# A gnn and mixture-of-experts kernel: tokens laid 32 to a partition, x loaded in five pieces, z made by two engines, rows filled in advance in longer runs

## The reference

```
z   = layernorm(x)
agg = adj @ z + beta[:, None] * z                  # adj is 4096 x 4096, float32, 64 MiB
x   = x + (agg / (sum(adj, axis=1) + beta)[:, None]) @ kernel + bias
z1  = layernorm(x)
logits = z1 @ Wr + br;  top 2 of 64;  gates = softmax of the two logits
x   = x + sum over the two: gate * (relu(z1 @ W1[e] + b1[e]) @ W2[e] + b2[e])
```

## Time and profile before

| | us |
|---|---|
| median of the three runs | 433.78 |
| the profiled execution | 433.03 |
| its span, first to last instruction | 431.2 |
| TensorE, VectorE, GpSimd, ScalarE busy | 359.3, 312.4, 250.3, 157.8 |

### The profile page before, as it was taken

One profiled execution on the slowest core, in us unless ns is written; L12 is line 12 of the kernel. 1 busy time (PEld: TensorE's weight loads), 2 busy tenths in 40 slices (PEclk: granted clock), 3 DMA queues, 4 the chain that ended last, 5 costly groups with the idle time before them and its releaser, 6 DMA issues.

```text
span 431.2 us, 8273 instructions
## 1 busy us (share of the span) xinstructions
PE 359.3 (83%) x2029; PEld 286.2 (66%) x2029; DVE 312.4 (72%) x891; ACT 157.8 (37%) x242; POOL 250.3 (58%) x226
## 2 busy tenths in 40 slices
PE   5899699996999999999899935289999999999300
PEld 2334486784786877868678632179999999999300
DVE  2699779859789798898897628246777767677257
ACT  1115185454384654845738030001222112122054
POOL 4377600308488585884857763517777777777700
PEclk8799899996999999999999975869999999999955
DMA  8998999899696996969955110479999999997189
GB/s 267 351 423 280 338 364 357 240 361 397 249 397 218 420 366 234 401 214 403 374 218 238 44 46 19 142 205 269 307 295 311 304 285 312 295 277 235 31 288 297
DMA packets 59653, 119.32 MB, mean 277 GB/s; under 512 B 7656, under 2 KB 36604, under 8 KB 51440
## 3 DMA queue, kind: packets, MB, share of 16 engines
q1 hardware_dynamic: 41968, 95.95, 63.8%
q10 hardware_dynamic: 12672, 14.58, 11.0%
q0 software_dynamic: 4992, 8.54, 5.5%
HBM read 104.09 MB, written 16.78 MB: 280 GB/s over the span
## 4 chain that ended last, share of the span: by engine, by line
PE 33%; POOL 19%; DVE 17%; DMA 15%; issue 10%; ACT 3%; SPq 1%; ACTq 0%; POOLq 0%; DVEq 0%
POOL dispatched_rows L451 14%; PE bank L897 8%; DMA dispatched_rows<-payload,slot 7%; PE bank L907 4%; PE bank_pair L907 4%; DVE z_sb L600 4%; DVE adj_low L615 3%; POOL diag L438 3%; DMA x_sb<-x 3%; DMA expert_answers<-adj_ring,ans 3%; PE bank L891 2%; PE bank L843 2%; PE bank L839 2%; PE bank_pair L904 2%; PE bank L840 2%
## 5 line engine op out<-in xcount | busy, mean ns | idle before, releaser
L615 DVE TENSOR_TENSOR adj_low<-adj_ring,adj_high 128x2048 fp32r<-128x2048 f32 x49 | 114.3, 2347 | 24.5 <-ACT adj_high L501 24.2
L451 POOL DMA_INDIRECT dispatched_rows<-payload,slot x64 | 95.7, 1495 | 37.8 <-issue 31.3
L501 ACT CAST adj_high<-adj_ring 128x2048 fp32r<-128x2048 f32 x49 | 93.4, 1907 | 60.7 <-PE bank L843 47.6
L470 POOL DMA_INDIRECT expert_answers<-adj_ring,ans x92 | 90.5, 983 | 41.4 <-ACT adj_ring L551 21.8
L839 PE MATMUL bank<-adj_high,z_hi 128*128 128x512 f32 x196 | 80.7, 412 | 0.0
L840 PE MATMUL bank<-adj_high,z_lo 128*128 128x512 f32 x196 | 77.5, 396 | 0.0
L749 DVE TENSOR_SCALAR adj_ring<-bank,adj_ring 128x128 f32<-128x128 f32 x184 | 56.1, 346 | 16.4 <-PE bank L897 13.2
L829 PE MATMUL bank<-adj_ring,z_sb 128*128 128x512 f32 x120 | 58.2, 629 | 5.5 <-DVE z_sb L600 5.3
L897 PE MATMUL bank<-xt_sb,adj_ring 128*128 128x128 f32 x368 | 57.6, 280 | 0.2 <-DVE xt_sb L739 0.2
L843 PE MATMUL bank<-adj_low,z_hi 128*128 128x512 f32 x196 | 53.5, 395 | 0.0
L897 PEld LDWEIGHTS bank<-xt_sb,adj_ring 128*128 128x128 f32 x368 | 49.7, 196 | 0.5 <-DVE xt_sb L739 0.5
(11 more groups left out here) (125 smaller groups left out, 452.8 us busy)
## 6 DMA issues: line engine op xcount, KB each, us to landing
adj_ring<-adj_t SPq DMA_DIRECT2D x64, 1024.0 KB, 8.4
adj_ring<-w_pack SPq DMA_DIRECT2D x48, 257.5 KB
adj_ring<-w_pack ACTq DMA_DIRECT2D x44, 257.5 KB
dispatched_rows<-pad_row SPq DMA_DIRECT2D x8, 528.0 KB, 9.8
adj_ring<-expert_answers SPq DMA_DIRECT2D x8, 512.0 KB, 7.3
adj_ring<-dispatched_rows SPq DMA_DIRECT2D x48, 66.0 KB
adj_ring<-dispatched_rows ACTq DMA_DIRECT2D x44, 66.0 KB
out<-x_sb SPq DMA_DIRECT2D x8, 256.0 KB, 5.2
```

Of the source, the lines that this page charges most:

```text
L451: pool.indirect_dma_start(rows, bass.IndirectOffsetOnAxis(ap=slot[:, b, i:i + 1], axis=0), payload[:, b, t, k, :], None).then_inc(scattere ...
L470: pool.indirect_dma_start(y_tok, bass.IndirectOffsetOnAxis(ap=ans[:, s:s + 1], axis=0), y_sb[:, s, :], None, bounds_check=N * K - 1, oob_i ...
L501: nc.scalar.copy(high[:, m % PARTS], adj_sb[:, slot_of(g, k)]).then_inc(hi_ready, 1)
L615: v.tensor_tensor(low[:, m % PARTS], adj_sb[:, slot_of(g, k)], high[:, m % PARTS].bitcast(F32), ALU.subtract).then_inc(lo_ready, 1)
```

## The change

A token is now `p * 32 + t`: each partition holds 32 tokens that follow one another in DRAM. x, beta, the answers and the output are read and written so, and the adjacency is laid out for it on the host (same runs of 8192 bytes). An expert's answer index follows (`answer_tab`).

x comes in five pieces of 4, 4, 8, 8 and 8 tiles (`BATCHES`), one run to a partition each. Pieces 1 and 2 are issued behind adjacency chunk 0, piece 3 behind chunk 1, piece 4 behind chunk 2. VectorE does statistics of piece b + 1 before the z of piece b. It makes the z of the first half of each piece, ScalarE that of the other half, from `rstd0` and `shift0`. VectorE no longer waits for `consts` at the start, and ScalarE takes one square root ahead of time, so that its table is loaded.

GpSimd no longer adds the bias to x. The bias is loaded into row 127 of a zeroed tile and added to the weight, whose last row meets the column of ones. The order of GpSimd's constants changes.

The rows filled in advance are now written in runs of eight (4224 bytes). Each of the eight DMAs covers 64 partitions, one to an expert, with two runs each, by turns from partitions 0 to 63 and 64 to 127. Their places among the chunks (`PADS`) stay.

```diff
+BATCHES = ((0, 4), (4, 4), (8, 8), (16, 8), (24, 8))
+X_BEFORE = (1, 3, 4, 5)
...
-            x_tiles = x.rearrange("(t p) f -> p t f", p=P)
-            sp.dma_start(x_sb[:, 0:GT], x_tiles[:, 0:GT]).then_inc(x_first, 16)
+            x_tiles = x.rearrange("(p t) f -> p t f", p=P)
+            def load_x(b):
+                first, count = BATCHES[b]
+                sp.dma_start(x_sb[:, first:first + count], x_tiles[:, first:first + count]).then_inc(x_in[b], 16)
+            load_x(0)
...
-                if k == 0:
-                    sp.dma_start(x_sb[:, GT:TILES], x_tiles[:, GT:TILES]).then_inc(x_in, 16)
+                if k < len(X_BEFORE) - 1:
+                    for b in range(X_BEFORE[k], X_BEFORE[k + 1]):
+                        load_x(b)
...
-                    sp.dma_start(gnn_b_sb[:], gnn_b.partition_broadcast(P)).then_inc(params_in, 16)
+                    sp.dma_start(gnn_b_sb[P - 1:P, :], gnn_b.partition_broadcast(1)).then_inc(params_in, 16)
...
-                        sp.dma_start(first_rows[:, padded:padded + EC],
-                                     pad_row[:, None, :].to_broadcast([P, EC, ROW])).then_inc(prefilled, 16)
+                        start = padded // PAD_BLOCKS % 2 * E
+                        sp.dma_start(blocks[:, padded:padded + PAD_BLOCKS],
+                                     pad_rows[start:start + E, None, :].to_broadcast([E, PAD_BLOCKS, PAD_RUN * ROW])).then_inc(prefilled, 16)
...
-            for g in range(GROUPS):
-                add_bias(g)
-                if g < SPLIT:
-                    low_z(g)
+            for g in range(SPLIT):
+                low_z(g)
+            pool.wait_ge(params_in, 16 * 5)
...
+            def make_z(b):
+                act.wait_ge(shift0, b + 1)
+                for t in act_half(b):
+                    nc.scalar.activation(z_sb[:, t, 0:D - 1], x_sb[:, t, 0:D - 1], ACT.Identity,
+                                         bias=shift0_sb[:, t:t + 1], scale=rstd0[:, t:t + 1]).then_inc(z_by_act, 1)
...
+            root_z(0)
+            for b in range(len(BATCHES)):
+                make_z(b)
+                if b + 1 < len(BATCHES):
+                    root_z(b + 1)
+                high_z(b)
...
+            spread_x(0)
+            for b in range(len(BATCHES)):
+                if b + 1 < len(BATCHES):
+                    spread_x(b + 1)
+                make_z(b)
...
+            own.after(v.tensor_tensor(gnn_wd[:, 0:D], gnn_w_sb[:], wrow_ps[:, 0:D], ALU.subtract))
+            v.tensor_tensor(gnn_wd[:, 0:D], gnn_wd[:, 0:D], gnn_b_sb[:], ALU.add).then_inc(wd_ready, 1)
```

More of the change, by code:

```diff
@@ L50, with batch_of, dve_half, act_half @@
 RING = 5
+BATCHES = ((0, 4), (4, 4), (8, 8), (16, 8), (24, 8))
+X_BEFORE = (1, 3, 4, 5)
 OUT_CH = 4
 OUT_STEPS = TILES // OUT_CH
+def batch_of(j):
+    return max(b for b, (first, _) in enumerate(BATCHES) if first <= j)
+def dve_half(b):
+    first, count = BATCHES[b]
+    return range(first, first + count // 2)
+def act_half(b):
+    first, count = BATCHES[b]
+    return range(first + count // 2, first + count)
+def z_made(j):
+    b = batch_of(j)
+    earlier = BATCHES[b][0] // 2
+    if j in dve_half(b):
+        return "dve", earlier + j - dve_half(b)[0] + 1
+    return "act", earlier + j - act_half(b)[0] + 1
 def chunk_no(g, k):
@@ L210, in program @@
         y_in = in_ring(TILES * K * D, "p (t k f) -> p t k f", t=TILES, k=K)
-        x_first = sem("x_first")
-        x_in = sem("x_in")
+        x_in = [sem(f"x_in{b}") for b in range(len(BATCHES))]
         params_in = sem("params_in")
@@ L346, in _ @@
             sp.wait_ge(consts, 1)
-            first_rows = rows.rearrange("(e s) c -> s e c", e=E)[0:P]
+            blocks = rows.rearrange("(e s r) c -> e s (r c)", e=E, r=PAD_RUN)
             padded = 0
@@ L399, in _ @@
             pool.memset(seen[:], 0.0)
-            pool.memset(eps_sb[:], EPS)
-            own.after(pool.memset(payload[:], 0.0))
-            pool.memset(pad_row[:, ANSWER:ANSWER + 1], float(NO_ANSWER))
+            own.after(pool.memset(payload[:, :, :, :, ANSWER + 1:ROW], 0.0))
             pool.affine_select(out=ident[:], in_=ident[:], compare_op=ALU.not_equal, fill=1.0, base=0,
@@ L786, in _ @@
             warm(14, spare_bank)
-            pe.wait_ge(consts, 1)
+            pe.wait_ge(z_ones, 1)
             def gnn(g):
```

117 lines of the change are left out of this document (65 added, 52 removed).

## The result

The changed kernel takes **420.57 us** (median of four executions, 419.54 to 421.76); the kernel before took 433.39 on the same chip. The ratio is 0.9705, 95% interval 0.9672 to 0.9738, so 12.8 us faster. The forecast was 418.0 with a range of 413.8 to 425.5. The profiled execution took 419.54 us, its span is 417.7 us, 13.5 less than before.

A forecast was written before the change was run, and what follows sets the result against it. Group 0 was bound by the layernorm, z and `diag` chain, later groups mostly by TensorE, group 2 by a late DMA chunk. Terms -8.9 - 1.2 - 4.9 - 0.8 = -15.8 us took 433.78 to 418.0 us, range 413.8 to 425.5.

The forecast's parts named there:

- Start unchanged: Group 0: TensorE's start stays at 9.48 us, first chunk at low clock until about 15.4, then own product at 39.8.
- Rival (c): Group 0: z makers and `z_lo` collide, TensorE ends at 44 us as now; 422 to 423 us in all, chance 0.09.
- The copy at 40.8: End of group 0: `agg_sb` copied at 40.8 us instead of 49.70, a gain of 8.9 us.
- Rival (b): Group 0: TensorE keeps high clock or x's piece 1 lands early; 3 us more off, 414.5 to 415.5, chance 0.10.
- Bias at nothing: Group 0: bias in the weight's last row costs one VectorE addition while idle, 0 us; uncovered 0.3.
- Group 1: Second gnn group: without the TensorE idleness before it, 27.3 to 27.5 us, so -1.2 us (0 to -1.4).
- Fillings at the adjacency's rate: Advance filling DMAs: 4224-byte runs go at 426 GB/s, 1.27 us for each DMA instead of 2.15.
- rival (a): Fillings stay at 2.15 us each and 1 to 2 us are queued; group 2 takes 34 us, total 422.5 to 425, chance 0.28.
- (d): Fillings, written 2.16 MB apart, get slower than before: 3.6 us each eats all the gain, 4.3 gives 439; chance 0.05.
- Group 2: Third gnn group: burst's third chunk late by 0.5 us instead of 3.1, clock holds; 28.0 for 32.95 us, -4.9.
- Group 3: Fourth gnn group: no change forecast from its 27.27 us, difference 0.
- End: Last stretch: longer runs for y's answers and out shorten the first load and last store, -0.8 us (0 to -2).

The follow-up runs named there:

- run 1: The changed kernel with the advance fillings again in 528-byte runs from 128 partitions, as before the change: 425.08 us, ratio 0.9804 to the kernel before.
- run 7: The changed kernel with ScalarE copying `agg_sb` of groups 0 and 1 before rounding the last look-ahead chunk, and fillings issued earlier: 418.59 us, ratio 0.9653.
- run 11: The changed kernel with all of z made by VectorE, none by ScalarE: 421.28 us, ratio 0.9691 to the kernel before.
- run 12: The changed kernel with x in two pieces of 4 and 28 tiles instead of five: 429.02 us, ratio 0.9909 to the kernel before.
- run 6: The changed kernel with ScalarE copying `agg_sb` of group 0 before rounding chunk 2 of group 1: 421.05 us, ratio 0.9693 to the kernel before.
- run 3: The changed kernel with VectorE making z of piece 0 before it waits for piece 1 of x: 421.55 us, ratio 0.9725 to the kernel before.
- run 4: The changed kernel with the eight bias additions on GpSimd again and no bias in the weight: 421.27 us, ratio 0.9725 to the kernel before.
- run 10: The changed kernel with all eight fillings read from partitions 0 to 63, without turns between halves: 421.01 us, ratio 0.9702 to the kernel before.
- run 9: The changed kernel with two fillings moved out of group 2's burst to earlier chunks: 419.29 us, ratio 0.9658 to the kernel before.
- run 8: The changed kernel with the edits of run 3 and run 7 together: 419.60 us, ratio 0.9661 to the kernel before.

## Why the prediction was right, step by step

*Start unchanged: right.* TensorE's first product came at 9.39 us (forecast 9.3 to 9.48), behind the wait for piece 1 of x, at the low clock to about 15.4, and then without idle time. The clock of that chunk was a matter of luck, since runs 1 and 7 start alike and have the full one; it did not matter, as run 1 shows. Own product 40.07, forecast 39.8. That z only has to keep up is shown by run 11 (one maker does). That an early z of the later tiles is what brings the 8 us is shown by run 12, but not that it takes five pieces. Rival (c), z still paces, is out.

*The copy at 40.8: 1.0 us too early.* This is the term that was mis-sized in group 0. I let ScalarE copy at once when TensorE was through. But it rounds three chunks of group 1 ahead of the copy, and the third one landed only at 40.0 to 41.5 us, since the DMA engines are full from 16 us on (429 GB/s in 16 to 20). My sum of bytes looked at group 0's chunks and not at the three of group 1 that stand ahead of the copy. The rows for it were there: in the earlier trace rows ScalarE waited 5.10 us for TensorE at this copy, so lateness of chunks had been hidden. Most of the 1.0 us is the low rate there: the chunk ahead was rounded from 36.62 on, and at 426 GB/s the third would have followed at 39.1 and the copy at 41.0 (an estimate), but in 32 to 40 us the engines move 363 and 337 GB/s, and why is open. That TensorE frees the slot earlier does not help: in run 1 the third chunk is issued at 32.4 and rounded at 39.88. Run 6 shows that taking the copy forward doesn't help: the same bytes are then missing later.

*Rival (b), a warm start worth 3 us: refuted* by run 3. It had the full clock and an earlier start, and TensorE waited for the third and fourth chunks; in run 1 the rival's own condition, the full clock in the first chunk, is met, and the own product comes 1.0 us earlier, the copy 0.1. My estimate that the adjacency keeps up (426 GB/s from 2 us on) was too high: the windows of 4 to 16 us show 381, 393 and 282. It did no harm to the forecast only because TensorE was slow at the time.

*Bias at nothing: right* as long as two engines make z (run 4: 0 to 1 us).

*Group 1: -1.35 for -1.2.*

*Fillings at the adjacency's rate: right.* 425 GB/s with two of them under way; run 1 shows the opposite case in the same kernel, 365 GB/s. So rivals (a) and (d) fail on their condition. The rule that I weighed, the Trainium skill's "SBUF — State Buffer", section "Door 1: The DMA port swizzle" (64 partitions reach half of the ports), does not show here, neither with turns between the halves nor from one half alone (run 10, 423 and 424 GB/s). The runs mix fillings with adjacency loads, so they show that nothing is lost in the mix, not what a filling alone would reach. The Trainium skill's "DMA: Bandwidth & Descriptors", section "Latency and other measured facts", has a padded row pitch at full rate again. The trace agrees, within the same mix: 64 runs 2.16 MB apart cost nothing there.

*Group 2: 28.62 for 28.0,* late by 1.2 us (mask wait 2.13, where the undisturbed ones are 0.84) and not by 0.5. From the burst's issue (68.24) to the rounding of its third chunk (83.17) it took 14.9 us, forecast 14.2. It was not the queue of 1 to 2 us that I had put into rival (a): the engines' share is 0.26 in 68 to 69 us. They move only 204 GB/s in 68 to 72 and 373 in 72 to 76, before they reach 423, so the burst started more slowly than my 2 us allow; why is open. ScalarE's wait for that chunk is 1.10 us, against the sign "none over 1 us". The wait for `mask` is 1.9 us shorter, and the rest of the 4.3 is the clock, which stayed up here and did not in four other profiles with the same wait.

*Group 3: +1.2, not foreseen.* This is what failed as a step: I treated the fillings as late only for the chunks behind them. GpSimd's first scatter also waits for all eight (`prefilled`), and it started at 85.42 us; GpSimd then frees `payload` for group 3 too late, ScalarE waits 1.72 us for it (107.90) and TensorE the same at `mask`. Run 9 moves two fillings, the first scatter starts at 79.62, and group 3 is back at 27.33, its wait at 0.86. Run 7 has the scatter at 75.03 and the same group 3. In the kernel before the scatter came at 96.85, later still behind group 1, but group 2 was so long that it stood 14.5 us ahead of the copy of group 2. The profiles fall into two sets by that distance: at 12.3 to 12.5 us (the changed kernel, twice, and runs 4 and 12) group 3 takes 27.9 to 28.6 us, at 13.9 or more 27.3 to 27.4. So a part of what group 2 gains below 30 us is handed back here: groups 2 and 3 together take 57.1 and 57.3 us in the two profiles of the changed kernel, and 57.6 to 57.7 in those of runs 3, 6, 10 and 11, whose clock fell in group 2.

*End: -1.05 for -0.8, of which only 0.6 can be shown:* 0.3 for the first answers and 0.3 for the last store. The rest lies in the expert stage, whose length varied between 160.4 and 162.3 us over the profiles with the same work there; what makes it vary is open.

Together: 1.0 + 0.6 + 1.2 of missing gain, less 0.15 in group 1 and 0.25 at the end, make up the 2.3 us between -15.8 and -13.5, to within rounding.

## What to carry to other kernels

When a stage is made earlier, count the bytes of everything that is queued ahead of its last hand-over, the next stage's look-ahead included: here DMA, not the maker of z, holds what a still earlier start would give (runs 3, 6 and 8 all came back with nothing). A transfer that nothing waits for at once, such as an advance filling, still has a deadline at the engine that checks it; spread it into the stretch where the DMA share is below 1 and look who waits on its semaphore. Run 9 shows that in the groups of one profile (2.2 us), not yet in the time. And let neither a big first load nor the statistics of all its tiles stand ahead of the first consumer: having both in run 12 cost 8.5 to 9.3 us, of which the share of the pieces alone is not known. Undoing the long runs cost some 4 us. Undoing the second maker of z or the moved bias, each with the other kept, cost nothing that can be measured; both at once were not undone. Run 7 (418.59 us) and run 9 (419.29) have the lowest medians, but their intervals overlap the changed kernel's, so neither is shown to be better.
